# State-space scan kernel on one core: chunk factors zero-padded to 128 rows, result matmuls in batches of eight, smaller DMA ring

## The reference

```python
xz = silu(in_proj_w @ gn(x) + b)            # 768 channels: x_ssm, res, gate
xf = silu(depthwise_conv3(x_ssm) + dw_b)
dbc = dbc_w @ xf + dbc_b                    # per head: dt, B_t (8), C_t (8)
# both heads: tokens permuted by an argsort of Moebius scores
h_t = exp(dt * A) * h_{t-1} + dt * B_t * x_t   # state: 8 per channel
y_t = C_t . h_t + D * x_t
# permuted back
out = x + silu(out_proj_w @ (y * silu(gate) + res) + b)
```

## Time and profile before

| | us |
|---|---|
| median of 3 runs | 1252.72 |
| the 3 runs | 1245.59, 1252.72, 1258.89 |
| profiled execution: span, first to last instruction | 1174.1 |
| PE busy in it | 961.5 (82%) |
| PEld / DVE / ACT / POOL busy | 597.9 / 588.0 / 579.1 / 532.4 |
| mean granted TensorE clock | 0.89 of full |

### The profile page before, as it was taken

One profiled execution on the slowest core, in us unless ns is written; L12 is line 12 of the kernel. 1 busy time (PEld: TensorE's weight loads), 2 busy tenths in 40 slices (PEclk: granted clock), 3 DMA queues, 4 the chain that ended last, 5 costly groups with the idle time before them and its releaser, 6 DMA issues.

```text
span 1174.1 us, 12950 instructions
## 1 busy us (share of the span) xinstructions
PE 961.5 (82%) x3988; PEld 597.9 (51%) x3988; DVE 588.0 (50%) x1104; ACT 579.1 (49%) x1078; POOL 532.4 (45%) x628
## 2 busy tenths in 40 slices
PE   1039666997899988998899779997999889978966
PEld 0035445664467445754476346744575357634643
DVE  5966136534572448444753348243853466345613
ACT  4824423345734564547444564456553754456341
POOL 0002527164555627371826545471936373644340
PEclk9558765798899998999899989998999899998987
DMA  8830290135912391247513491238313661348122
GB/s 331 331 120 1 81 157 1 36 119 155 216 36 93 101 226 71 72 133 183 140 37 121 144 213 48 78 101 192 121 63 122 179 162 37 119 152 148 37 94 86
DMA packets 112051, 142.54 MB, mean 121 GB/s; under 512 B 41705, under 2 KB 91122, under 8 KB 111986
## 3 DMA queue, kind: packets, MB, share of 16 engines
q1 hardware_dynamic: 99698, 105.91, 34.0%
q0 software_dynamic: 12288, 35.80, 9.4%
HBM read 88.07 MB, written 53.61 MB: 121 GB/s over the span
## 4 chain that ended last, share of the span: by engine, by line
PE 41%; DMA 21%; POOL 16%; issue 10%; DVE 5%; SPq 4%; ACT 3%; POOLq 0%; ACTq 0%; DVEq 0%
PE pj L1183 12%; POOL xt_scratch L389 10%; PE pj L1258 9%; PE pj L1256 8%; DMA xb<-in_x 7%; DMA cd_scratch<-xp 6%; POOL big L401 4%; SPq L302 4%; PE st L1230 3%; DMA xp<-xt_scratch 2%; DMA xt_scratch<-stage,idx 2%; PE tp L1241 2%; PE tp L1206 2%; DMA crow<-cd_scratch 2%; POOL big L413 2%
## 5 line engine op out<-in xcount | busy, mean ns | idle before, releaser
L1183 PE MATMUL pj<-xb,wsc 128*128 128x512 f32 x768 | 392.1, 658 | 39.0 <-DMA xb<-in_x 26.6
L413 POOL TENSOR_TENSOR big<-big,crow 128x128 f32<-128x128 f32 x256 | 182.1, 751 | 212.6 <-DMA crow<-cd_scratch 199.1
L1183 PEld LDWEIGHTS pj<-xb,wsc 128*128 128x128 f32 x768 | 155.0, 213 | 205.9 <-issue 197.7
L389 POOL DMA_INDIRECT xt_scratch<-stage,idx x128 | 139.6, 1091 | 83.0 <-DVE stage L941 46.4
L358 POOL TENSOR_SCALAR wsc<-inw,pcur 128x256 f32<-128x256 f32 x96 | 62.6, 669 | 239.1 <-PE pj L1183 150.7
L401 POOL DMA_INDIRECT big<-yt_scratch,idx x128 | 130.5, 1020 | 75.5 <-issue 37.7
L1258 PE MATMUL pj<-ch 64*128 64x128 f32 x512 | 129.2, 333 | 0.0
L1256 PE MATMUL pj<-xp,mblk 128*128 128x128 f32 x512 | 120.1, 318 | 4.2 <-ACT xs L519 4.2
L1304 PE MATMUL pj<-gt,outw 128*128 128x512 f32 x256 | 111.8, 594 | 0.1
L995 DVE TENSOR_TENSOR_SCAN hs<-big,st 128x64 f32<-128x64 f32 x256 | 49.0, 265 | 101.8 <-PE st L1230 101.8
L570 ACT COPY ch<-tp 128x256 f32<-128x256 f32 x128 | 45.4, 376 | 106.6 <-PE tp L1242 106.6
(11 more groups left out here) (192 smaller groups left out, 1348.7 us busy)
## 6 DMA issues: line engine op xcount, KB each, us to landing
xb<-in_x SPq DMA_DIRECT2D x32, 1024.0 KB, 7.4
xp<-xt_scratch SPq DMA_DIRECT2D x8, 2048.0 KB, 10.0
crow<-cd_scratch SPq DMA_DIRECT2D x128, 128.0 KB, 7.8
yt_scratch<-rs SPq DMA_DIRECT2D x16, 1024.0 KB, 4.4
out<-xb SPq DMA_DIRECT2D x16, 1024.0 KB, 10.2
xp<-xt_scratch SPq DMA_DIRECT2D x8, 272.0 KB, 3.5
xt_scratch<-stage,idx POOLq DMA_INDIRECT x128
big<-yt_scratch,idx POOLq DMA_INDIRECT x128, 2.7
```

Source lines behind the costliest of these rows:

```text
L389: pool.indirect_dma_start(out=xt_d.ap(), out_offset=bass.IndirectOffsetOnAxis(ap=idx[:, k:k + 1], axis=0), in_=v(stage, (nt * H + h) * ROW ...
L413: last = nc.gpsimd.tensor_tensor(v(big, W_OFF + (s * Q + b * NT) * L, (L, NT), (1, L)), v(big, s * EEW + SEG + b * NT * L, (L, NT), (1, L) ...
L1183: last = nc.tensor.matmul(o[:, :], v(wsc, (b * CT + ct) * 2 * C + slot * C + ot * P, (1, P)), x_view(par, b, ct, nt * HALF, HALF), start=( ...
```

## The change

The C factors get a width of 128 columns a tile: an even tile's 64 columns are followed by 64 zeros, an odd tile's are preceded by 64 zeros (`cblk` is cleared once at the start, and two VectorE instructions of half the size write into it). `turn` now turns the two padded tiles and the states: three transposes a unit in place of two, and ScalarE's copy takes 384 columns in place of 256. The matmul that adds the states' part reads all 128 partitions; the zeros take out the other tile's states. `result` is split in two: `within` (the `mblk` matmuls, four tiles a call) and `from_states` (eight matmuls of one image in a row). `AHEAD` stays 2 for ScalarE's program. The scratch for dynamic DMAs is set to 8192 bytes a partition, smaller than before; `cblk` and `ch` take 6 KB a partition more.

```diff
-        cblk = sb("cblk", Q * CPT * S)
+        cblk = sb("cblk", Q * P)
-        ch = sb("ch", 4 * 2 * P)
+        ch = sb("ch", CH * 3 * P)
...
-                    nc.scalar.copy(v(ch, (u % CH) * 2 * P, (1, 2 * P)), v(tp[u % 2], 0, (1, 2 * P))).then_inc(t_drained, 1)
+                    nc.scalar.copy(v(ch, (u % CH) * 3 * P, (1, 3 * P)), v(tp[u % 2], 0, (1, 3 * P))).then_inc(t_drained, 1)
...
+            nc.vector.memset(v(cblk, 0, (1, Q * P)), 0.0)
...
-                nc.vector.tensor_tensor(v(cblk, 0, (CPT * S, Q), (S, CPT), (1, S)), v(bc8, CS, (S, Q), (0, CPT), (1, S)),
-                                        const("chunk", (0, Q), (1, CPT), (0, S)), ALU.mult).then_inc(cblk_ready, 1)
+                for e in range(2):
+                    last = nc.vector.tensor_tensor(
+                        v(cblk, e * (P + CPT * S), (2 * P, Q // 2), (S, CPT), (1, S)),
+                        v(bc8, CS + e * S, (2 * S, Q // 2), (0, CPT), (1, S)),
+                        const("chunk", (0, Q // 2), (1, CPT), (0, S)), ALU.mult)
+                last.then_inc(cblk_ready, 1)
...
-                nc.tensor.transpose(v(o, 0, (1, P)), v(cblk, (b * NT + 2 * gp) * CPT * S, (1, P)), const("ident"))
-                nc.tensor.transpose(v(o, P, (1, P)), v(hs, (b * (NC + 1) + 2 * gp * CPT) * S, (1, P)), const("ident")).then_inc(t_full, 1)
+                for e in range(2):
+                    nc.tensor.transpose(v(o, e * P, (1, P)), v(cblk, (b * NT + 2 * gp + e) * P, (1, P)), const("ident"))
+                nc.tensor.transpose(v(o, 2 * P, (1, P)), v(hs, (b * (NC + 1) + 2 * gp * CPT) * S, (1, P)), const("ident")).then_inc(t_full, 1)
...
+            def within(i, h, b, tiles, before):
+                if tiles[0] == 0:
                     pj_slot(2 * b + 1, None, None, before)
                     pe.wait_ge(mblk_ready, i * H + h + 1)
+                for g in tiles:
+                    gp, e = divmod(g, 2)
+                    nc.tensor.matmul(v(pj[2 * b + e], gp * P, (1, P)), v(mblk, (b * NT + g) * P, (1, P)), x_rows(h, b, g),
+                                     start=(gp == 0), stop=False, skip_group_check=True)
+            def from_states(i, h, b):
+                for gp in range(4):
+                    u = h * 8 + b * 4 + gp
+                    pe.wait_ge(t_drained, i * T_U + u + 1)
+                    for e in range(2):
+                        last = nc.tensor.matmul(v(pj[2 * b + e], gp * P, (1, P)), v(ch, (u % CH) * 3 * P + e * P, (1, P)),
+                                                v(ch, (u % CH) * 3 * P + 2 * P, (1, P)), start=False, stop=True,
+                                                skip_group_check=True)
+                    last.then_inc(ch_used, 1)
             def results(i, h, before_t, before_r, turned_before=0, between=None):
-                for k in range(8):
-                    if k + AHEAD < 8:
-                        turn(i, h, k + AHEAD, before_t)
-                    result(i, h, k, before_r)
-                    if k == 3 and between:
-                        between()
+                for b in range(NB):
+                    within(i, h, b, range(0, 4), before_r)
+                    turn(i, h, 4 * b + 2, before_t)
+                    turn(i, h, 4 * b + 3, before_t)
+                    within(i, h, b, range(4, 8), before_r)
+                    from_states(i, h, b)
+                    if b == 0:
+                        turn(i, h, 4, before_t)
+                        turn(i, h, 5, before_t)
+                        if between:
+                            between()
...
-    nc = _bacc.Bacc("TRN2", target_bir_lowering=False, num_devices=1)
+    nc = _bacc.Bacc("TRN2", target_bir_lowering=False, num_devices=1, dynamic_dma_scratch_size=8192)
```

More of the change, by code:

```diff
@@ L94, in build @@
         cd_d = nc.dram_tensor("cd_scratch", [H * N, S * NB], F32)
+        CH = 4
         cst = sb("cst", CONST_W)
@@ L202, in build @@
         X_U, T_U, Y_U = NB * NT, H * NB * NT // 2, NB * H * 2
-        CH = 4
         AHEAD = 2
@@ L1260, in result @@
-                last.then_inc(ch_used, 1)
+                for g in tiles:
[11 more added lines that the diff above has]
+                    last.then_inc(ch_used, 1)
@@ L1262, in results @@
             def results(i, h, before_t, before_r, turned_before=0, between=None):
-                for k in range(turned_before, AHEAD):
+                for k in range(turned_before, 2):
                     turn(i, h, k, before_t)
-                for k in range(8):
-                    if k + AHEAD < 8:
-                        turn(i, h, k + AHEAD, before_t)
-                    result(i, h, k, before_r)
-                    if k == 3 and between:
-                        between()
+                for b in range(NB):
[9 more added lines that the diff above has]
+                            between()
```

## The result

| | before | after |
|---|---|---|
| median, same chip | 1255.33 (1245.59 to 1258.89) | 1157.08 (1151.31 to 1159.98) |
| ratio, 95% | | 0.9228 [0.9179, 0.9276] |
| profiled execution: time, span | span 1174.1 | 1151.31, 1149.5 |

The account below looks back on a forecast made before the run. One serial loop per phase, with the result matmuls on it, was taken as the bound. Gains of 11.2 (phase 0), 47.0 (phases 1, 2, 4, 5, 6), 8.9 (phase 3) and 10.5 (phase 7) made 77.6: 1175 us, range 1163 to 1190.

Parts of the forecast that it names:

- The sum: Whole kernel: the phases' gains make 77.6 us, 78.6 us around the span stays, so 1252.7 becomes 1175 us.
- Phase 0: at half the clock I take 0.22 a record: Head 0's results in phase 0, clock staying at half: 17.9 us against 24.6, a gain of 6.7.
- Result matmuls, all with 128 rows: Result sections: 0.115 us a record; head 0 from 14.28 to 9.34 us, head 1 from 15.23 to 10.0 before waits.
- the rival by which the matmul fills the distance: Result matmuls: the matmul itself, not the border, takes 0.155 us a record; 41 us gained, 1212 us; chance 0.12.
- the slower one, no gain per record: Result matmuls: records stay at 0.209 us and the third transpose is paid; 15 us slower, 1268 us; chance 0.05.
- The wait that the new order adds: Head 1's results: TensorE waits some 0.7 us for ScalarE's copy of unit 6, so head 1 gains 4.5.
- What comes late next: GpSimd's first scatter: its wait for `stage` caps head 1's gain at 4.0 us in phase 3, no cap elsewhere.
- GpSimd has no slack: GpSimd's gathers start or end later, swallowing head 1's gain in phases 0 to 6; 1206 us; chance 0.05.
- The other edits: Split `cblk` writes cost one more start; its clear is hidden, else 2.3 us once; the smaller ring costs nothing.
- That rival: Smaller DMA ring fills: each indirect DMA of seven phases up to 1.44 us longer, 1498 us at most; chance 0.04.

Follow-up runs that it names:

- 128 rows by turns: Changed kernel's padded 128-row data, but token and states' matmuls by turns as in the kernel before: 0.9336 on a quick chip, 0.9178 on a slow one.
- batches: Kernel before with the new order in both heads, states' matmuls over 64 partitions, two transposes a unit: 0.9034 on a quick chip, 0.9296 and 0.9235 on slow ones.
- batches in head 0 alone: Kernel before with the new order over 64 partitions in head 0 only: 1187.29 us against 1251.19, ratio 0.9504, on a slow chip.
- with pairs in head 1: Kernel before, 64 partitions: head 0 in batches of eight, head 1 with each unit's token matmuls before its states' matmuls: 0.9181 quick chip, 0.9094 slow chip.
- small ring: Kernel before with only the scratch for dynamic DMAs set to 8192 bytes: 1.0014 on a quick chip, 0.9939 on a slow one.
- batches in head 1 alone: Kernel before with the new order over 64 partitions in head 1 only: 1236.23 us against 1251.19, ratio 0.987, on a slow chip.
- pairs: Kernel before, in both heads each unit's two token matmuls first, then both states' matmuls over 64 partitions: 1166.26 us against 1251.19, ratio 0.9299, slow chip.

## Why the forecast was wrong, by its steps

**"The sum", its last step, failed: "what lies around it, 78.6 us to the median of the runs, stays".** 1.8 us lie around a span. The 78.6 were the difference between a page of kind A and runs of kind B. By luck little came of it: the ratio is the same on both, so a gain in per cent (77.6 of 1174.1, 6.6%) would have given 1170 for kind B. That is 5 of the 18 us between 1175 and 1157.

**"Phase 0: at half the clock I take 0.22 a record" failed too, and was the mis-sized term of the gain.** Stretches of phase 0 with before on kind A (head 0, chunk sums, head 0) and then with the changed kernel on kind A:

```profile
184.85:197.44 12.59, 12.59 (x39) 9.00 (x39) 11.37 (x12) 1.12 (x3) 12.59 (x15) 0.50 0.00 0
197.44:200.84 3.40, 3.40 (x17) 3.40 (x17) 0.00 (x0) 1.07 (x2) 1.73 (x4) 0.50 0.02 5
200.84:213.06 12.22, 12.22 (x38) 8.63 (x38) 8.23 (x11) 0.74 (x2) 0.00 (x0) 0.50 0.00 1
```

```profile
184.75:191.64 6.89, 6.89 (x45) 6.89 (x46) 6.71 (x9) 1.09 (x3) 6.89 (x10) 0.71 0.00 0
191.64:193.37 1.73, 1.73 (x18) 1.73 (x17) 1.73 (x2) 1.71 (x4) 1.73 (x2) 1.00 0.04 9
193.37:197.65 4.28, 4.28 (x40) 4.28 (x40) 4.21 (x5) 0.86 (x2) 4.28 (x5) 1.00 0.01 2
```

The section starts at the same time in both, after a wait, at the 1.2 GHz level. In the changed kernel the granted clock goes to the 2.4 GHz level within the first stretch and stays; before it stayed at 0.50 through all three. The forecast had taken the level for fixed. It gives 24.81 - 11.17 = 13.6 us for the 6.7 of the forecast, 1.7 more in the chunk sums and 1.9 in the projection behind (8 records in 3.60 us for 5.50). From phase 0's load of sorted rows to phase 1's there are 135.2 us with before and 114.1 with the change: 21.1, where the sum had 11.2. That is 10 of the 11.6 us by which the spans differ from the forecast on kind A (1171.7 - 1082.5 = 89.2 for 77.6). Which form lifts the clock could be read off the other kernels: it rises in this section in all forms with few crossings or none (changed, 128 rows by turns, batches, batches in head 0 alone or with pairs in head 1), on both kinds, and stays at 0.50 in all with 16 or 32 (before, small ring, batches in head 1 alone, pairs). By its records PE is busy for 100% of the stretch in both; what differs is PEld, 9.00 of 12.59 and 6.89 of 6.89. The wait just ahead of the section isn't what counts: it is 4.2 us in before and 3.9 with 128 rows by turns, where the clock rises.

On kind B, where the result was measured, the same term was off in the same way. Before with the small ring and the changed kernel, on one chip, differ by 13.3 us in head 0 of phase 0 (6.7 in the sum) and by 16.6 from phase 0's load of sorted rows to phase 1's (11.2). Phases 1 to 6 differ by 60.5 there (55.9) and phase 7 by 12.5 (10.5).

**"Result matmuls, all with 128 rows": right.** 0.22 a pair against 0.23 said, transposes 0.11, head 0 9.17 for 9.34, and head 1 in the shape that was described. That rules out the rival by which the matmul fills the distance (0.155 a record), and the slower one, no gain per record. PEld is busy 4.28 of 4.28 us beside PE. So the sentence of the Trainium skill (TensorE: Matmul & The Clock Gate, The mechanism) that loads overlap matmuls in flight only where the row group differs doesn't hold for these 128x128 float32 matmuls.

**"The wait that the new order adds": right.** Changed kernel on kind A, phase 1: ScalarE's copies, results and silu, and TensorE's wait.

```profile
333.50 0.86 ACT L570 COPY ch<-tp 128x384 f32<-128x384 f32 x2 [2.48 <-PE tp L1248]
334.25 1.09 ACT L580 COPY rs<-pj 128x512 f32<-128x512 f32 x2
335.20 2.22 ACT L526 ACTIVATE xf<-xf,small 128x1024 f32<-128x1024 f32 x2
337.29 0.88 ACT L570 COPY ch<-tp 128x384 f32<-128x384 f32 x2
337.84 1.16 PE L1266 MATMUL pj<-ch 128*128 128x128 f32 x8 [0.71 <-ACT ch L570]
```

0.71 for the 0.7 said, in this order of ScalarE's work. Head 1 is 10.75 for 10.7.

**"What comes late next": right on kind A.** The first scatter waits 1.0 to 1.1 in six phases and 2.0 in one, where the slack of 4.0 to 5.5 was to be used up to 0 to 1. Batches over 64 partitions use it up. Phases 1 to 6 gave 57.2 us together (55.9 in the sum), phase 7 and what follows it 10.5 (10.5), and 0.4 lay before phase 0's load. The rival "GpSimd has no slack" falls with it. On kind B the step doesn't hold: the first scatter comes 1.1 us closer there for 4.4, and by the distances (14.9 us down to 9 to 12) the output projection comes 3 to 6 us a phase closer to the last scatter.

**"The other edits": right where it was tested.** The indirect DMAs still come every 1.26 us (602.29 to 631.46 are 23 steps of 1.27), and the ring alone is no loss. That rival falls too. The two writes of `cblk` and the clear weren't tried alone; the section starts of phase 0, 184.75 and 184.85, show no cost of theirs.

## What to carry to other kernels

Price a matmul by its neighbours: where 64- and 128-partition matmuls take turns, each change costs some 0.2 us here that neither record shows. Sorting them by shape was worth more than padding them to one shape on kind A (0.9034 for 0.9244) and not on kind B (0.9235 and 0.9296 for 0.922 to 0.923). Set a sum made from one profiled execution only against that execution's own time, or carry it over as a ratio (0.922 to 0.924 on both kinds here, though from different places): the distance to another chip's median is no constant. After a wait, ask whether another form of a stretch would lift TensorE's clock, as that gain comes on top and reaches into what follows; and time a reordering on more than one chip, since the best order differed between two kinds here.

## What the runs showed of the hardware that was not expected

- Two kinds of chip: the same kernel takes 1171 to 1190 us on two and 1246 to 1275 on four. On the latter, in the stretch of GpSimd's indirect DMAs, VectorE stands in single waits of up to 12.6 us (after) and 16.1 (before with the small ring) that nothing on the core ends by the trace, and ScalarE in some too. Whether those DMAs cause it is open, and so is whether a chip keeps its kind.
- Sixteen float32 records over alternating halves of the rows take 0.068 us each, in couples that start 0.007 apart; sixteen over all rows take 0.11 each (1.95 us for 16, 1.79 to the next start).
- In phase 0 the granted clock rose in the first stretch of head 0 for kernels with few changes of shape, and not before the projection behind head 0 for those with many, at a PE busy share of 100% in both.
- No version came out best on both kinds: batches over 64 partitions in both heads win on kind A (0.9034), batches in head 0 with pairs in head 1 on kind B (0.9094 [0.9042, 0.9146]). The latter is on neither kind behind the changed kernel (0.9181 for 0.9244 on the same chip of kind A; 0.9094 for 0.922 to 0.923 on kind B, other chips), with two transposes a unit and the full ring.
